# Cross-attention's values weighed batch by batch in 32-row groups of the array, one PSUM bank per batch, with one VectorE transpose for the probabilities

## The reference, cut to what matters

```python
q = split_heads(layernorm(x) @ w_q)          # 16 heads of 64
k = split_heads(ctx @ w_k)
v = split_heads(ctx @ w_v)
scores = einsum('bhqd,bhkd->bhqk', q, k) * 64 ** -0.5
scores += (k_pos > q_pos) * -10000.0         # causal
weights = softmax(scores)
out = einsum('bhqk,bhkd->bhqd', weights, v)  # the part that is changed
x = x + out.reshape(...) @ w_o
x = x + self_attention(layernorm(x))         # 16 heads of 16
x = x + ffn(layernorm(x))                    # gate, up, down with 4-bit blockwise rounding
```

## Time and profile before

| | before |
|---|---|
| median of 3 runs | 627.73 us (627.31 to 629.44) |
| the profiled execution | span 627.5 us, from its first to its last instruction |
| PE busy, share of the span | 554.8 us, 88% |
| DVE busy | 531.7 us, 85% |
| ACT busy | 207.2 us, 33% |
| cross-attention stage | 0 to about 306.5 us |
| rows `L348` (`weigh`), matmul records | 512, 32.6 us busy |
| rows `L534` (`turn_probs`) | 64, 44.8 us busy |

### The profile page before, as it was taken

How to read it: one execution, slowest core, us unless ns; L and a number is a source line. 1 busy time by engine, 2 the same in 40 slices (tenths; PEclk the granted TensorE clock), 3 DMA queues, 4 the chain that set the end, 5 groups by cost and what they waited for, 6 DMA issues and landing times.

```text
span 627.5 us, 16121 instructions
## 1 busy us (share of the span) xinstructions
PE 554.8 (88%) x6390; PEld 434.1 (69%) x6390; DVE 531.7 (85%) x1067; ACT 207.2 (33%) x429; POOL 45.0 (7%) x84
## 2 busy tenths in 40 slices
PE   4999999999999999997448888888899888888885
PEld 4888888888888888885335656666676666666553
DVE  5868999999999999998256889999999998999984
ACT  1323323322333323321025444443444433443120
POOL 4001000000000000000011110011111101101100
PEclk9999999999999999999758979999999998999898
DMA  8990111211101111121000000000000000000000
GB/s 253 328 303 3 67 67 67 67 67 67 67 17 51 67 67 67 67 67 69 4 0 3 1 3 9 8 8 8 0 8 8 8 8 8 8 8 8 10 9 17
DMA packets 13798, 30.97 MB, mean 49 GB/s; under 512 B 976, under 2 KB 10704, under 8 KB 11728
## 3 DMA queue, kind: packets, MB, share of 16 engines
q1 hardware_dynamic: 13776, 30.67, 15.1%
HBM read 28.57 MB, written 2.10 MB: 49 GB/s over the span
## 4 chain that ended last, share of the span: by engine, by line
issue 30%; DVE 10%; PE 6%; ACT 2%; POOL 2%; DVEq 0%; POOLq 0%; ACTq 0%
PE bank L1123 2%; DVE f_xn L1348 2%; PE bank L1101 1%; POOL f_rstd L1014 1%; DVE f_xn L1449 1%; DVE f_amax_x L1446 1%; PE bank L1145 1%; ACT a_kblocks L1245 1%; DVE f_pow_x L1462 1%; DVE f_pow_x L1457 1%; DVE f_h L1366 1%; DVE f_inv_x L1448 1%; DVE f_amax L1374 1%; PE bank L1071 0%; PE bank L1168 0%
## 5 line engine op out<-in xcount | busy, mean ns | idle before, releaser
L316 PEld LDWEIGHTS bank<-x_xcT,xwk 128*128 128x128 f32 x512 | 61.0, 196 | 2.8 <-issue 1.1
L316 PE MATMUL bank<-x_xcT,xwk 128*128 128x128 f32 x512 | 61.4, 279 | 1.4 <-ACT x_xcT L408 1.4
L357 PE MATMUL bank<-xwo,x_oT 128*128 128x256 f32 x256 | 59.5, 387 | 1.1 <-ACT x_oT L425 1.1
L338 PE MATMUL bank<-xwv,x_xcT 128*128 128x512 f32 x128 | 59.2, 605 | 1.2
L307 PE MATMUL bank<-x_xcT,xwq 128*128 128x128 f32 x512 | 59.8, 275 | 0.0
L307 PEld LDWEIGHTS bank<-x_xcT,xwq 128*128 128x128 f32 x512 | 58.5, 192 | 0.0
L357 PEld LDWEIGHTS bank<-xwo,x_oT 128*128 128x128 f32 x256 | 48.6, 195 | 7.9 <-issue 1.6
L1101 PE MATMUL bank<-wdT,f_hqT 128*128 128x256 f32 x192 | 47.4, 398 | 3.0 <-ACT f_hqT L1221 3.0
L1245 ACT ACTIVATE a_kblocks<-bank,head_rows 128x256 f32<-128x256 f32 x128 | 48.6, 499 | 0.0
L534 DVE STREAM_TRANSPOSE x_probsT<-x_probs 32x512 f32<-32x512 f32 x64 | 44.8, 701 | 1.7
L437 ACT COPY x_k_blocks<-bank 64x512 f32<-64x512 f32 x32 | 18.6, 581 | 79.9 <-PE bank L316 79.7
(11 more groups left out here) (152 smaller groups left out, 966.5 us busy)
## 6 DMA issues: line engine op xcount, KB each, us to landing
x_ctx_slab<-in_ctx_dram SPq DMA_DIRECT2D x16, 1028.0 KB, 4.8
out_dram<-f_out SPq DMA_DIRECT2D x16, 128.0 KB, 1.7
xall<-in_x_dram SPq DMA_DIRECT2D x1, 1280.0 KB, 17.3
x_first_keys<-in_ctx_dram SPq DMA_DIRECT2D x4, 320.0 KB, 12.5
xwk<-in_L_xattn_w_k_dram SPq DMA_DIRECT2D x1, 1024.0 KB, 5.0
xwq<-in_L_xattn_w_q_dram SPq DMA_DIRECT2D x1, 1024.0 KB, 7.1
xwv<-in_L_xattn_w_v_dram SPq DMA_DIRECT2D x1, 1024.0 KB, 10.3
xwo<-in_L_xattn_w_o_dram SPq DMA_DIRECT2D x1, 1024.0 KB, 12.8
```

The source lines that it names most:

```text
L316: last = nc.tensor.matmul(bank[2 + j // 4][:, (j % 4) * P:(j % 4 + 1) * P], xwk[:, k, j * P:(j + 1) * P], xcT[:, KD + k, :], start=(k == 0 ...
L338: last = nc.tensor.matmul(bank45[:, half, :], xcT[:, KD + k, :], xwv[:, k, half * 512:(half + 1) * 512], start=(k == 0), stop=(k == KD - 1))
L357: last = nc.tensor.matmul(bank67[:, 0, 0:D], oT[:, j, :], xwo[:, j, :], start=(j == 0), stop=(j == XP - 1))
```

## The change

`weigh` now issues one matmul for each head and each batch: 64 instead of 16. Each takes 32 rows of `v` (the batch's keys, 64 columns) as the loaded operand and 32 moving columns, at `tile_position=(b * SQ, half)`, and writes to a bank of its own per batch: banks 2, 3, 4 and 5, which are now one tensor `bank2345`. `pT` shrinks to 128 x 16 x 32 without zero blocks, its memset goes, and `turn_probs` becomes one transpose of 128 x 512 (which VectorE does in 32 x 32 blocks). As banks 2 and 3 hold the keys' projection of tile t+1 until both halves of `spread_k(t+1)` have read it, `weigh(t)` gets two more waits. `copy_o` gathers from four banks.

```diff
-        bank = [ctx.enter_context(nc.psum_tensor(f"bank{i}", [P, 512], F32)) for i in range(4)]
-        bank45 = ctx.enter_context(nc.psum_tensor("bank45", [P, 2, 512], F32))
+        bank = [ctx.enter_context(nc.psum_tensor(f"bank{i}", [P, 512], F32)) for i in range(2)]
+        bank2345 = ctx.enter_context(nc.psum_tensor("bank2345", [P, 4, 512], F32))
+        bank += [bank2345[:, 0, :], bank2345[:, 1, :]]
+        bank45 = bank2345[:, 2:4, :]
...
-            pT = psb("probsT", [P, H, P])
-            oT = psb("oT", [P, XP, P])
+            pT = psb("probsT", [P, H, SQ])
+            oT = psb("oT", [P, XP, BT, SQ])
...
-                    def weigh(t):
+                    def weigh(t, spread):
                         pe.wait_ge(s_p, t + 1)
                         pe.wait_ge(s_vc, t + 1)
+                        if spread is not None:
+                            pe.wait_ge(s_kc, spread + 1)
+                            pe.wait_ge(s_kca, spread + 1)
+
                         for h in range(H):
                             j, half = h // 2, (h % 2) * XD
-                            last = nc.tensor.matmul(bank45[half:half + XD, j // 4, (j % 4) * P:(j % 4 + 1) * P],
-                                                    v[:, h * XD:(h + 1) * XD], pT[:, h, :],
-                                                    start=True, stop=True, tile_position=(0, half))
+                            for b in range(BT):
+                                rows = slice(b * SQ, (b + 1) * SQ)
+                                last = nc.tensor.matmul(bank2345[half:half + XD, b, j * SQ:(j + 1) * SQ],
+                                                        v[rows, h * XD:(h + 1) * XD], pT[rows, h, :],
+                                                        start=True, stop=True, tile_position=(b * SQ, half))
                         last.then_inc(s_o, 1)
...
-                        weigh(t)
+                        weigh(t, t + 1)
...
-                        nc.scalar.copy(oT[:].rearrange("p (a j) n -> p a (j n)", a=2), bank45[:]).then_inc(s_oc, 1)
+                        nc.scalar.copy(oT[:].rearrange("p j b q -> p b j q"),
+                                       bank2345[:, :, 0:XP * SQ].rearrange("p b (j q) -> p b j q", q=SQ))\
+                            .then_inc(s_oc, 1)
...
                     def turn_probs():
-                        for b in range(BT):
-                            rows = slice(b * SQ, (b + 1) * SQ)
-                            step(nc.vector.transpose(pT[rows, :, rows], pr[rows, :, :]))
-                        dve.sem_inc(s_p, 1)
+                        nc.vector.transpose(pT[:], pr[:]).then_inc(s_p, 1)
...
-                    nc.vector.memset(pT[:], 0.0)
```

More of the change, by code:

```diff
@@ L356, in output @@
                         for j in range(XP):
-                            last = nc.tensor.matmul(bank67[:, 0, 0:D], oT[:, j, :], xwo[:, j, :],
-                                                    start=(j == 0), stop=(j == XP - 1))
+                            last = nc.tensor.matmul(bank67[:, 0, 0:D], oT[:, j].rearrange("p b q -> p (b q)"),
+                                                    xwo[:, j, :], start=(j == 0), stop=(j == XP - 1))
                         last.then_inc(s_y, 1)
@@ L388, in _ @@
                     project_q(T - 1)
-                    weigh(T - 2)
+                    weigh(T - 2, T - 1)
                     scores(T - 1)
@@ L392, in _ @@
                     output(T - 2)
-                    weigh(T - 1)
+                    weigh(T - 1, None)
                     pe.wait_ge(s_reach, 1)
@@ L574, in _ @@
                     start = Chain(dve, s_ln, 3 * len(PARTS))
-                    step = Chain(dve, s_d, 2 + 1 + 3 + BT)
+                    step = Chain(dve, s_d, 2 + 1 + 3)
                     slab_step = Chain(dve, s_dc, 1)
```

## The result

The changed kernel takes 621.17 us in the median (620.63 to 621.54) against 627.65 us for the kernel before beside it: a ratio of 0.9874, 95% interval 0.9846 to 0.9902. It is faster, by 6.5 us where 17.7 were forecast. The profiled execution took 621.4 us, its span is 619.9, against a span of 627.5 before. What follows compares the two profiled executions.

A forecast was written before the change was run, and what follows sets the result against it. TensorE and VectorE were taken to bound the loop at nearly equal height. Gains of 11.25 us from the loop, 2.8 from a shorter stand and 3.6 from the last tile gave 17.7, so 610.0 us, range 607 to 615.5.

The forecast's parts named there:

- fifteen weighings: `weigh` of tiles 0 to 14 on TensorE's path, each 0.75 us shorter: 11.25 us gained.
- What bounds the kernel: Cross-attention's loop: TensorE 17.75 us a tile, VectorE 17.70; shortening VectorE alone gains nothing there, TensorE alone at most 0.05.
- the loop's code, 96 to 144 matmuls, being fetched again in each turn: Cross-attention's loop: named as the example of "anything else", chance 0.03, with no size given.
- The matmuls' pace: In `weigh`: eight tiles overlap at 7.7 to 8.5 ns per record, the group taking 1.17 to 1.27 us against 1.97.
- rival 1: In `weigh`: only four tiles overlap, each group 0.15 us longer, 3.9 us gained in all, 623.8 us; chance 0.18.
- rival 2: In `weigh`: loads into the same 64 columns don't overlap, each group 2.1 us longer, 655 us; chance 0.14.
- A floor of 25 ns: In `weigh`: matmul starts never under about 25 ns apart; if binding between row groups, 644 us; chance 0.02 within 0.14.
- VectorE: One transpose of 128 x 512 takes 0.70 us against 2.90 for four; VectorE's tile becomes 15.5 us.
- the new waits: `weigh(t)` waits for `spread_k(t+1)`, expected done 2.1 us early, so costing nothing in the loop.
- if the cover were gone: At the waits for `spread_k`: without the spare 1.4 and 2.1 us, each microsecond late costs TensorE one.
- `copy_o`: ScalarE's copy after `weigh`, now in pieces of 32: loss between nothing and 2.6 us in all, taken as nothing.
- The end of the stage: Last tiles of cross-attention: TensorE stands 0.6 us instead of 3.4, keeping full clock; 2.8 and 3.6 us gained.

The follow-up runs named there:

- TensorE's part alone: Changed kernel with its 64 matmuls kept, but VectorE transposing batch by batch in four chained instructions as before: 635.21 us, ratio 1.0098.
- VectorE's alone: Kernel before with one transpose of 128x512 in place of four and the old weighing, whose sums are then not the reference's: 623.23 us, ratio 0.9896.
- The shifts by 16, 28 and 64: Changed kernel with that many small matmuls added ahead of the loop, 28 and 64 also with FFN and self-attention weights sent later: 619.31, 619.77, 619.18 us.
- the version with pairs: Against the changed kernel, two batches share 64 rows, giving 32 matmuls with 64 moving columns: 622.28 us; with FFN and self-attention weights sent later, 615.97 us.
- the late transfers: Changed kernel with the FFN's and self-attention's weight transfers waiting until the first weighing is done: 619.68 us, ratio 0.9831.
- the run with row groups in turn: Changed kernel with the weighing's 64 matmuls ordered one batch after the other, all heads inside, so two tiles are in use at a time: 675.14 us.
- half the columns: Changed kernel's weighing with 32 loaded and 16 moving columns instead of 64 and 32 for 14 of 16 heads: 622.58 us.

## Why the prediction was wrong

Of the 11.2 us between 610.0 and 621.17, 9.7 lie at the last residual, 0.4 behind it, and 1.1 in the step from the span to the median, taken as 0.2 us and measured as 1.3. The predicted 17.7 us at the last residual against 305.04 - 297.06 = 7.98 measured, term by term:

| | predicted | measured |
|---|---|---|
| fifteen weighings | 11.25 (0.75 each) | 7.35 (0.49 each) |
| from `output(14)` on | 6.4 | 6.2 |
| first turn of the loop | 0 | -4.62 |
| clock in the first projection | 0 | -1.07 |
| left open | 0 | 0.12 |

- **What bounds the kernel** was read rightly: two engines at one height, neither part worth its own price in the loop. TensorE's part alone made the kernel slower, VectorE's alone kept 17.75 us a tile.
- **The step that failed** is "the loop's code, 96 to 144 matmuls, being fetched again in each turn", put at 0.03 under "anything else" and at nothing in the sum. The question was put wrongly: the code isn't fetched in each turn, but once, and TensorE waits at a boundary in it if it gets there before the code. Before the change the same boundary lay, by count, near the end of `output(0)` (from 40.31 us), long after its packet had moved (35.4 to 36.7 us); the change put 96 more pairs of weight load and matmul ahead of it, and the boundary came into the first weighing. The shifts by 16, 28 and 64 and the version with pairs, whose 64 records fewer put it at record 59 of the scores, show the place; the late transfers show the part of the DMA engines. It cost 3.0 us as a stop and 1.6 as the fallen clock behind it.
- **The matmuls' pace** is the second step, right in kind and 3.9 us too good in size. The group is 1.49 us, not the 2.1 of rival 1 or the 4.0 of rival 2. That all eight tiles are in flight at once isn't measured: with the 48.8 ns that a tile takes for a record in the run with row groups in turn, 10.0 ns are 4.9 tiles in the mean. I took 7.7 to 8.5 ns per record from the load's round and it is (1490 - 225)/127 = 10.0; with half the columns it is 8.55 outside the one gap. The row that gave 8.5 had 17 moving columns and four tiles, and I let the middle of a range go below the fastest row.
- **A floor of 25 ns** between starts shows in neither order. The Trainium skill (TensorE: Matmul & The Clock Gate, section "Wait — 56ns, not 53.3ns?") gives the figure without saying on how many tiles. Over eight tiles it is 10.0 ns here; with two it is 24.4 in the mean, but most starts there are 6 and 52 ns apart in turn.
- **VectorE**, 0.70 us, and **the new waits**, nothing in the loop, were right (the keys' projection ends 3.5 us ahead of `weigh`, not 3.57, which changes nothing); that the latter cost TensorE 0.46 us a tile as soon as VectorE is slower is what the price "if the cover were gone" stood for. **`copy_o`** keeps its 1.01 us. **The end of the stage** came within 0.2 us, full clock included, and partly by luck: TensorE stood 0.24 us instead of 0.6, as its later arrival left VectorE more time, while `weigh(15)` took 0.27 us more than predicted, the way to `output(15)` 0.17 and `output(15)` 0.10.

## What to carry to other kernels

Where a change multiplies small instructions, count code as well as time: look where the first pass through a loop, and the code behind it, meets the next packet of instructions, and whether DMA engines are full just then. Take the pace of tiny matmuls from the group with as many instructions, not from the width of their loads, and try half as many of twice the size: here that took the group from 1.49 to 1.16 us, and paid once the stop was gone as well. When two engines run at one height, measure each part alone: one may be the whole gain and the other a loss.

## What the runs showed of the hardware

- Float32 matmuls on different row groups of one column strip, each with a PSUM bank of its own, overlap, weight loads included: 10.0 ns per record over eight tiles of 32 x 64, 24.4 ns over two, 14.9 ns over four of 64 x 64.
- Going from tiles of 64 columns to tiles of 32 within a group cost one gap of 148 ns between starts, in each of the 16 weighings of the run with half the columns.
- In the run with row groups in turn TensorE never paused, and yet its clock fell behind each weighing: the windows of one tile show a granted clock of 0.72 in the 6 us behind it, the lower level (1.2 GHz) for part of them, with TensorE busy throughout. What brings the clock down there is open.

```profile
99.20:102.50 3.30, 3.30 (x131) 3.22 (x130) 2.12 (x5) 1.01 (x1) 0.00 (x0) 1.00 0.00 0
102.50:108.60 6.10, 6.10 (x75) 3.46 (x73) 4.17 (x6) 1.64 (x2) 0.00 (x0) 0.72 0.00 0
```

- Stops for code are placed to the record, and their places come back every 64 float32 matmuls. In the first turn, in a burst of small matmuls, one costs 0.85 and 1.18 us of idle time with free DMA engines, 1.57 to 4.29 with full ones; behind the loop 1.40 and 1.48. The two versions in which it is nearly gone (0.08 us) or short (0.45) have late transfers as well. Where long matmuls surround the place, as in the kernel before, none shows.
